# Top-32 attention: the mask tables of each batch move from VectorE to GpSimd

## The reference

```python
q = (query @ Wq.T + bq).reshape(Bn, Sq, H, DK).transpose(0, 2, 1, 3)     # H = 16 heads of DK = 16
k = (key @ Wk.T + bk).reshape(Bn, -1, H, DK).transpose(0, 2, 1, 3)
v = (value @ Wv.T + bv).reshape(Bn, -1, H, DK).transpose(0, 2, 1, 3)
scores = jnp.einsum('bhqd,bhkd->bhqk', q, k) / jnp.asarray(np.sqrt(DK), (scores_dtype := q.dtype))
scores = jnp.where(mask[:, None] == 0, jnp.asarray(NEG, scores.dtype), scores)   # NEG = -1e9
vals, idx = jax.lax.top_k(scores, 32)
p = jax.nn.softmax(vals, axis=-1)
vg = jnp.take_along_axis(v[:, :, None, :, :], idx[..., None], axis=3)
ctx = jnp.einsum('bhqk,bhqkd->bhqd', p, vg)
x = ctx.transpose(0, 2, 1, 3).reshape(Bn, Sq, Dm)
return x @ Wo.T + bo
```

## Time and profile before

| | us |
|---|---|
| median of 3 runs | 2441.24 (2434.01 to 2441.58) |
| the profiled execution, its own time | 2440.11 |
| its span | 2438.3 |
| VectorE busy in the span | 1604.2 |
| GpSimd busy | 951.7 |
| TensorE busy, ScalarE busy | 1987.9, 1183.1 |
| mean granted TensorE clock, of full speed | 0.825 |

### The profile page before, as it was taken

The page is one execution under the profiler, slowest core; times in us unless marked ns, Lnnn a source line. Parts: engine busy times, 40 slices in busy tenths (PEclk is TensorE's granted clock), DMA queues, the critical chain, the costliest instruction groups (busy, mean ns, idle before and its releaser), DMA issues. The chain is left out here.

```text
span 2438.3 us, 40723 instructions
## 1 busy us (share of the span) xinstructions
PE 1987.9 (82%) x13441; PEld 1621.2 (66%) x13441; DVE 1604.2 (66%) x5274; ACT 1183.1 (49%) x3293; POOL 951.7 (39%) x919
## 2 busy tenths in 40 slices
PE   8985999599948967976999947777878778777888
PEld 5663898499937855655999935566656666665555
DVE  6776111588974237854111168999999999995786
ACT  3544232455421115543333325687777787875444
POOL 3311454300007023303555425666666666662210
PEclk9997999655779989987999965577777678757899
DMA  3112565520315012315354330000000000101442
GB/s 97 62 47 84 205 240 177 150 37 1 108 48 182 0 65 74 101 36 184 130 205 161 106 123 25 1 31 18 31 18 31 31 1 31 49 1 63 164 157 77
DMA packets 101861, 204.50 MB, mean 84 GB/s; under 512 B 20158, under 2 KB 70550, under 8 KB 93718
## 3 DMA queue, kind: packets, MB, share of 16 engines
q1 hardware_dynamic: 77568, 116.19, 14.3%
q0 software_dynamic: 23808, 85.50, 10.2%
q10 hardware_dynamic: 280, 0.23, 0.0%
HBM read 216.24 MB, written 55.28 MB: 111 GB/s over the span
## 5 line engine op out<-in xcount | busy, mean ns | idle before, releaser
L833 DVE MATCH_REPLACE8 l3a_left<-l3a_top,l3a_left 128x256 f32<-128x256 f32 x768 | 308.3, 409 | 0.0
L826 DVE MAX8 l3a_top<-l3a_left 128x8 f32<-128x256 f32 x768 | 285.5, 413 | 0.0
L525 POOL TENSOR_TENSOR l3a_prob<-l3a_expd,l3a_rest 128x512 f32<-128x512 f32 x128 | 162.8, 1272 | 211.4 <-ACT l3a_rest L608 210.4
L363 PEld LDWEIGHTS l3a_psO<-l3a_probT,l3a_vp 128*128 128x128 f32 x1024 | 185.5, 269 | 69.7 <-ACT l3a_probT L624 40.6
L363 PE MATMUL l3a_psO<-l3a_probT,l3a_vp 128*128 128x128 f32 x1024 | 210.0, 370 | 24.7 <-ACT l3a_probT L624 24.6
L345 PE MATMUL l3a_psT<-all_ident,l3a_prob 128*128 128x128 f32 x512 | 112.8, 361 | 106.0 <-POOL l3a_prob L525 105.2
L512 POOL TENSOR_TENSOR l3a_kept<-l3a_raw_sc,l3a_mone 128x512 f32<-128x512 f32 x128 | 163.7, 1279 | 71.9 <-ACT l3a_raw_sc L592 67.9
L2043 ACT ACTIVATE l2f_hT<-l2f_psH,l2f_wt 128x128 f32<-128x128 f32 x312 | 89.2, 369 | 209.8 <-PE l2f_psH L1997 209.8
L518 POOL TENSOR_TENSOR l3a_sc_sb<-l3a_kept,l3a_mlow 128x512 f32<-128x512 f32 x128 | 164.1, 1282 | 10.0
L345 PEld LDWEIGHTS l3a_psT<-all_ident,l3a_prob 128*128 128x128 f32 x512 | 80.0, 186 | 123.9 <-POOL l3a_prob L525 123.4
L2403 PE MATMUL dtw_psS<-dtw_r,all_shift 128*128 128x1 f32 x596 | 152.7, 356 | 10.2 <-DVE dtw_r L2583 9.8
(11 more groups left out here) (599 smaller groups left out, 4730.4 us busy)
## 6 DMA issues: line engine op xcount, KB each, us to landing
key_at<-l3a_a_k SPq DMA_DIRECT2D x8, 768.0 KB, 3.3
kv_at<-dtw_vd SPq DMA_DIRECT2D x8, 512.0 KB, 2.8
k_at<-dtw_kx SPq DMA_DIRECT2D x8, 512.0 KB, 4.2
l1f_kx<-k_at SPq DMA_DIRECT2D x8, 512.0 KB, 4.5
kv_at<-l1f_k SPq DMA_DIRECT2D x8, 512.0 KB, 3.2
l2a_k<-kv_at SPq DMA_DIRECT2D x8, 512.0 KB, 5.6
l2a_vd<-kv_at SPq DMA_DIRECT2D x8, 512.0 KB, 6.6
l2f_yb<-rows_y SPq DMA_DIRECT2D x8, 512.0 KB
```

The source lines that it names most:

```text
L363: mm = nc.tensor.matmul(psO[y % 2][:, c, 0:P], vp[:, p, kc, c, g * P:g * P + P], probT[:, u % 2, kc, e, :], start=(j == 0 and e == 0 and k ...
L525: nc.gpsimd.tensor_tensor(prob[:, u % 4, :, :], expd[:, u % 2, :, :], rest[:, u % 2, :, :], ALU.subtract).then_inc(picked, 1)
L826: ins = nc.vector.max(top[:, e, eight], rows[:, e, :] if r else scores[:, e, :])
L833: ins = nc.vector.match_replace(out=rows[:, e, :], in_to_replace=top[:, e, eight], in_values=rows[:, e, :] if r else scores[:, e, :], imm_ ...
```

## The change

`read_mask` moves from VectorE's program to GpSimd's. For batch 0 it runs there after the memset and before the first caps, and for batch b + 1 at the start of n = 3 of batch b, ahead of `pick` of unit n = 2. The second table is now made from the first (`mlow >= 0`) instead of from the mask, with a new semaphore `m_low` between them. VectorE's loop loses the call.

```diff
@@ -185,6 +185,7 @@
+        m_low = s.sem("m_low")
@@ -518,6 +519,15 @@
+            def read_mask(b):
+                pool.wait_ge(m_in[b % 2], 16 * (b // 2 + 1))
+                if b >= 2:
+                    pool.wait_ge(capped, STEPS * (b - 1))
+                raw, one, low = (a[:, b % 2, :, :].rearrange("p q n -> p (q n)") for a in (mraw, mone, mlow))
+                nc.gpsimd.tensor_scalar(low, raw, 0.0, NEG, ALU.is_equal, ALU.mult).then_inc(m_low, 1)
+                pool.wait_ge(m_low, b + 1)
+                nc.gpsimd.tensor_scalar(one, low, 0.0, 1.0, ALU.is_ge, ALU.mult).then_inc(m_cap, 1)
+
@@ -525,9 +535,12 @@
+            read_mask(0)
             cap_scores(0)
             cap_scores(1)
             for i in range(U):
+                if i % STEPS == 3 and i // STEPS + 1 < B:
+                    read_mask(i // STEPS + 1)
                 if i >= 1:
                     pick(i - 1)
                 if i + 2 < U:
@@ -803,14 +816,6 @@
-            def read_mask(b):
-                dve.wait_ge(m_in[b % 2], 16 * (b // 2 + 1))
-                if b >= 2:
-                    dve.wait_ge(capped, STEPS * (b - 1))
-                raw, one, low = (a[:, b % 2, :, :].rearrange("p q n -> p (q n)") for a in (mraw, mone, mlow))
-                nc.vector.tensor_scalar(low, raw, 0.0, NEG, ALU.is_equal, ALU.mult)
-                nc.vector.tensor_scalar(one, raw, 0.0, 1.0, ALU.not_equal, ALU.mult).then_inc(m_cap, 1)
-
@@ -876,7 +881,6 @@
-            read_mask(0)
@@ -887,8 +891,6 @@
-                if b + 1 < B and n == 1:
-                    read_mask(b + 1)
```

## The result

| | before | the change |
|---|---|---|
| median of 9 runs, us | 2439.85 (2434.01 to 2441.58) | 2447.64 (2443.12 to 2454.83) |
| span of the profiled execution, us | 2438.3 | 2452.7 |

The account below looks back on a forecast made before the run. VectorE's instruction stream was taken to set the pace. Batch gains of 0.67, 0.67, 1.1, 1.1, 0, 0 and 0.2 sum to 3.7 us; 2440.1 became 2436.4, and with 1.1 us to the median 2437, range 2430 to 2444.

Parts of the forecast that it names:

- the price of the added work: Two GpSimd tensor_scalar and a semaphore wait per batch ahead of unit 2's pick: 1.65 us, costed at 0 as idle time covers it.
- C: Time of one pair of table instructions on GpSimd, put at 1.4 to 2.8 us, with 1.65 us taken.
- What is removed: Eight pairs of table instructions leave VectorE; the seven inside the attention stage sum to 8.7 us, the gain's upper bound.
- The pairs: The two VectorE instructions making each batch's mask tables, read as costing 0.66 to 2.54 us a pair.
- the mutual hold-up of the two engines: VectorE's table instruction and a GpSimd tensor_tensor slow each other: 1.50 us for 0.42, and 1.46 for 1.27.
- The first pair before the loop: The eighth pair, ahead of the first unit: worth nothing, since VectorE later waits 1.63 us for ScalarE's square roots.
- The cover on GpSimd: GpSimd's idle time before unit 2's pick, 1.45 to 2.58 us, hides the added pair until it passes about 2.5 us.
- The chain behind line 850: After n = 3 VectorE needs sums turned by TensorE and read by ScalarE; waits some 5 us in all, batches 2 to 6.
- hidden price: The added GpSimd pair, taken at 1.65 us, fits into idle time ahead of unit 2's pick and costs 0.
- The slack of each batch: Room before VectorE waits at line 850: 2.0 us in batch 1, about 1.1 in batch 2, 0.04 in batch 4.
- Batch 0: No line 850 at unit 3; a 7.1 us DMA stall at unit 6 moves along with VectorE, so gain 0.67 us.
- The rival of the other side: Slower by the tables' price: the late pick delays line 850, mean C − 2.8 us over six batches; chance 0.10.

Follow-up runs that it names:

- e2: The changed kernel with both tables made by mult and add instead of comparisons, still at n = 3; 2430.9 us, ratio 0.9977 to before.
- e10: e5 with the table of ones made by min from the int32 mask and the other from it by mult and add; 2431.6 us, ratio 0.9971.
- e6: The changed kernel with only the first table made by mult and add, the second still by a comparison; 2442.4 us, ratio 1.0003 to before.
- e1: The changed kernel with the tables moved from unit n = 3 to n = 6 of a batch; 2432.5 us, ratio 0.9985 to before.
- e3: The kernel before without the tables of batches 2 to 7 and their mask loads, nothing added on GpSimd; 2431.3 us, ratio 0.9975.
- e9: The changed kernel with tables at n = 6 and ScalarE's read of the turned sums ahead of the transposes' copy; 2433.0 us, ratio 0.9973.
- e5: e2 with ScalarE's read of the turned sums moved ahead of the transposes' copy and the next batch's queries; 2429.1 us, ratio 0.9957.
- e8: The kernel before, tables on VectorE, with ScalarE's read of the turned sums moved ahead of the transposes' copy; 2441.7 us, ratio 1.0010.

## Why the prediction was wrong, by its steps

**The step that failed: the price of the added work.** The prediction has "the price lies between rows", C from 1.4 to 2.8 us, 1.65 taken "since these are one-input instructions". Measured 3.94. The added work was costed at 0; against e2, which is the same kernel at C = 1.32, it brought 12.5 us of waits of line 855 (15.5 and 3.0). The bounds weren't bounds. I had looked for rows of the same engine, shape and instruction name, and all of these were mult and add; int32 input and constants differed too, but e2 shows that only the operations mattered, and they make a factor of 3.1 (e2, e10). I wrote down that no comparison existed in the trace, and then closed the range at the slowest arithmetic row. The trace of before also had a sign that I passed over, GpSimd's tensor_scalar at line 1450, which adds first and multiplies second:

```profile
L1450 POOL TENSOR_SCALAR l0a_xn<-all_x,l0a_nmean,all_rstd 128x256 f32<-128x256 f32 x16 | 8.8, 560 | 9.5 <-DVE all_rstd L115 9.5
```

That is 0.56 us for half the elements of the rows at 0.69 and 0.77. GpSimd's tensor_tensor takes 0.73 us at this size (line 1527) and 1.27 at the full one, so some 0.19 us of an instruction are fixed, which makes line 1450 an estimate of 0.93 us at the full size: arithmetic in another order already was dearer.

**What is removed: right.** The pairs gave back 7.7 us in batches 1 to 6 and 0.67 in batch 0, against 8.7 in before; the mutual hold-up of the two engines went with them. It wasn't confined to the long pairs: in batches 4 and 6 of before, where the pair was short, GpSimd's instruction beside it was stretched, to 1.89 us (start 1852.86) and 1.79 (2042.89) from 1.27. In the change no tensor_tensor of the stage takes over 1.3 us but one of 1.40 in batch 0. The first pair before the loop was worth nothing: VectorE's wait for the square roots behind it went from 1.63 to 3.83 us.

**The cover on GpSimd: right up to its edge.** "The cover is gone when C passes about 2.5 us." At 1.32 (e2) it holds, at 2.63 (e6) the waits have risen by 2.7 us, at 3.94 by 12.5.

**The chain behind line 850: right in kind, not batch by batch, and the place of the whole result.** Predicted "some 5 us in all" of waits with a hidden price; e1 and e2 show 3.1 and 3.0, e3 5.9. The slack of each batch was taken from one execution as if it belonged to the batch. For batch 5 the forecast was a gain of 0, and e2 gained 2.3 us there, half of its 4.7 in batches 1 to 6 (3.1 forecast): in before ScalarE was 4.4 us late at n = 1 of batch 5, in e2 2.4, with a granted clock of 0.70 and 0.75 in the units n = 13 and 15 ahead of it in before and of 0.70 and 1.00 in e2. At the price that I had taken, the forecast of 3.7 us less would have stood, if in part by luck: e2 is 5.6 us faster (interval 3.2 to 8.3).

**Batch 0: wrong by a little.** The gain of 0.67 went into the stall on the DMA, 7.8 us after 7.1. Later kernels show that this stall moves by more than that with no difference in the code ahead of it (4.2 us in e1, 7.4 in e9).

**The rival of the other side: right in mechanism and rate.** C − 2.8 a batch gives 6 × (3.94 − 2.8) = 6.8 us; measured 7.8, of which 2.8 are in batch 2 alone. It had a chance of 0.10, and of its price I said "no row shows" it. The Trainium skill's rule on branching (GPSIMD Engine Reference, section on elementwise cycle accounting), an estimate of 5.1 us an instruction, would have been too high; 1.93 us is measured, and no run shows whether these instructions branch. The same section's best case for a loop without such branching, 0.77 us, was too high too for mult and add with constants (0.62).

## What to carry to other kernels

The price of an instruction on another engine is only known from a row with the same operation; engine, shape and name aren't enough, and where no such row exists the range has to stay open on the dear side, or the price is measured first. On an engine with idle time, an added instruction is judged by what stands behind it: the same 3.9 us brought 12.5 us of waits ahead of the pick of unit 2 and none three units later. And taking work off the engine that sets the pace moves the wait to whoever is read in a fixed order behind it; here the 3.0 us that were left went with one line of ScalarE's order (e5). The slack of one batch in one trace is no property of that batch.

## What the runs showed of the hardware that I had not expected

- GpSimd tensor_scalar, 128 x 512 to float: mult with add of two constants 0.62 us; is_equal, is_ge, is_gt or min with mult 1.92 to 1.93 us; int32 input and float input the same.
- The stall on the DMA in batch 0 goes with the granted TensorE clock 24 to 39 us after the first max of the stage, while TensorE makes the next batch's keys and values, whose end lets SyncE issue the loads. The clock was 0.89 of full speed in e1, e2 and e5, with stalls of 4.0 to 4.4 us, 0.77 in e8 with 5.3, and 0.71 to 0.74 in the other eight with 6.3 to 8.1. e1 and e9 run the same code up to there (the last number but two is the clock):

```profile
1483.40:1498.40 15.00, 10.48 (x52) 7.93 (x52) 15.00 (x64) 10.18 (x34) 14.59 (x11) 0.89 0.03 9
```
```profile
1478.80:1493.80 15.00, 10.52 (x35) 7.76 (x35) 15.00 (x64) 9.26 (x30) 14.62 (x11) 0.71 0.00 1
```

Their stalls are 4.2 and 7.4 us, so the same code gave or took 3 us here, with another granted clock ahead of the stall.
- On VectorE and GpSimd side by side, either one can be the one that is stretched: tensor_scalar on VectorE from 0.42 to 1.50 us, or tensor_tensor on GpSimd from 1.27 to 1.89.
